# Splitting the second layer's messages into bf16 parts in a PSUM bank instead of in SBUF

## The reference

```python
Fj = features[src]                                  # gathered rows, 32 wide
R = relu(dist[:, None] @ w1 + b1) @ w2 + b2         # weights of every edge
acc += norm * einsum('euv,ef,evi,ofi->euo', Rb[..., k], Yf, Fb, C)
msg = concatenate(msg_blocks, axis=-1)
out = zeros(...).at[dst].add(msg)                   # sum at the destination
x = layernorm(x + out)
```

## Time and profile before

| | |
|---|---|
| median of 3 runs | 4053.04 us (4050.44 to 4053.18) |
| profiled execution | 4059.36 us |
| its span, first to last instruction | 4057.4 us |
| TensorE matmul busy | 3377.3 us (83%) |
| VectorE busy | 3460.9 us (85%) |
| GpSimd busy | 2953.0 us (73%) |
| ScalarE busy | 2184.8 us (54%) |
| GpSimd, gathers of the second layer | 1483.2 us in 1540 steps |
| VectorE, the 782 multiplies of the second layer | 832.4 us |

### The profile page before, as it was taken

How to read it: one execution, slowest core, us unless ns; L and a number is a source line. 1 busy time by engine, 2 the same in 40 slices (tenths; PEclk the granted TensorE clock), 3 DMA queues, 4 the chain that set the end, 5 groups by cost and what they waited for, 6 DMA issues and landing times. The chain is left out here.

```text
span 4057.4 us, 95500 instructions
## 1 busy us (share of the span) xinstructions
PE 3377.3 (83%) x23156; PEld 1945.7 (48%) x23156; DVE 3460.9 (85%) x5277; ACT 2184.8 (54%) x6587; POOL 2953.0 (73%) x3087
## 2 busy tenths in 40 slices
PE   4777777777777777777559999999999999999996
PEld 3444444444444444444335555555555555555553
DVE  8888888888888888888759999889889888988887
ACT  3555555555555555555335565555555555555554
POOL 5777777777777777777377777777777777777772
PEclk7888888888888888888779999999999999999998
DMA  3111111111111111111212222222221222222221
GB/s 107 35 33 32 34 32 33 34 33 35 32 33 32 33 32 34 36 32 33 35 38 48 45 44 44 44 44 44 47 45 41 47 44 44 44 43 44 44 44 28
DMA packets 238827, 162.68 MB, mean 40 GB/s; under 512 B 143937, under 2 KB 212594, under 8 KB 238066
## 3 DMA queue, kind: packets, MB, share of 16 engines
q1 hardware_dynamic: 104338, 91.78, 8.7%
q0 software_dynamic: 98560, 50.66, 8.6%
q10 hardware_dynamic: 35650, 17.88, 1.7%
HBM read 148.83 MB, written 10.43 MB: 39 GB/s over the span
## 5 line engine op out<-in xcount | busy, mean ns | idle before, releaser
L430 POOL DMA_INDIRECT rows<-x_rows,src x1540 | 1483.2, 963 | 536.6 <-issue 526.6
L430 POOL DMA_INDIRECT rows<-in_x,src x1540 | 1468.9, 954 | 485.6 <-issue 472.3
L775 PE MATMUL red<-prod,ident 128*128 128x336 f32 (+1 forms) x4704 | 1511.2, 475 | 1.4 <-DVE prod L1073 1.2
L775 PEld LDWEIGHTS red<-prod,ident 128*128 128x128 f32 x4704 | 892.3, 195 | 635.4 <-issue 193.3
L1073 DVE TENSOR_TENSOR prod<-wps,arena 128x896 f32<-128x896 f32 x782 | 832.4, 1083 | 176.2 <-PE wps L762 159.0
L755 PE MATMUL wps<-bias_parts,ones 64*128 64x448 bf16 (+1 forms) x2346 | 471.4, 398 | 610.7 <-DVE prod L1067 452.4
L565 ACT ACTIVATE gap<-iota,slot_plan 128x128 bf16<-128x128 f32 x3136 | 935.6, 386 | 7.0
L762 PE MATMUL wps<-w_sb,hidden 64*128 64x448 f32 (+1 forms) x3920 | 746.9, 476 | 0.0
L583 ACT ACTIVATE arena<-red 128x336 f32<-128x336 f32 (+1 forms) x294 | 135.5, 461 | 1103.5 <-PE red L775 1102.9
L755 PEld LDWEIGHTS wps<-bias_parts,ones 64*128 64x128 bf16 x2346 | 114.6, 94 | 1135.3 <-DVE prod L1067 562.4
L1082 DVE TENSOR_REDUCE arena<-prod 128x384 f32<-128x3072 f32 (+1 forms) x195 | 520.9, 2671 | 0.1
(11 more groups left out here) (127 smaller groups left out, 3025.3 us busy)
## 6 DMA issues: line engine op xcount, KB each, us to landing
mlp<-in_dist SPq DMA_DIRECT2D x196, 256.0 KB
fetched<-in_x SPq DMA_DIRECT2D x3072, 0.1 KB
fetched<-x_rows SPq DMA_DIRECT2D x3072, 0.1 KB
mlp<-in_feat SPq DMA_DIRECT2D x98, 256.0 KB
rows<-in_x,src POOLq DMA_INDIRECT x1540
rows<-x_rows,src POOLq DMA_INDIRECT x1540
frames<-frame ACTq DMA_DIRECT2D x49, 144.0 KB
geo<-frames ACTq DMA_DIRECT2D x98, 72.0 KB
```

The costliest lines, as they stand in the source:

```text
L430: nc.gpsimd.indirect_dma_start(out=rows[z][:, t, :], out_offset=None, in_=table_rows, in_offset=bass.IndirectOffsetOnAxis(ap=src_sb[z][:, ...
L775: ins = nc.tensor.matmul(red[:, bank * 512:bank * 512 + cols], ident[:], pr[:, i, :, a:b, :], start=(i == 0), stop=(i == MUL - 1))
```

## The change

For the second layer, except in the last round, the splits go through a PSUM bank. ScalarE copies the complete message into the bank `cut_ps` (512 columns, the whole of `acc`), VectorE subtracts the upper half in place there, ScalarE copies what is left to SBUF with a rounding to bf16 (`middle`, now the second part), and VectorE subtracts that from the bank to give the last part. ScalarE gains two copies a chunk and VectorE keeps two subtractions, of other operands. The scattered sums of the second layer move from `acc` to 128 free columns of the second bank of `red`; hence the scatter waits until both banks of sums are copied, and the second sum of products waits until the windows are split. In VectorE's order the first split moves from between windows 0 and 1 to behind multiply 6, and the second from behind multiply 6 to behind the projection, in the last round too (there they work in SBUF as before). The first layer keeps its order and its buffers.

```diff
+        red_end = 512 + (PE_SUMS[1][1][1] - PE_SUMS[1][1][0]) * PATHS[1] * MUL
+        acc_of = (acc[:, 0:GROUPS * FEAT], red[:, red_end:red_end + GROUPS * FEAT])
+        cut_ps = acc[:].rearrange("p (t f) -> p t f", t=TILES)
...
+        def middle(z):
+            return rest[z][:].bitcast(BF16)[:, :, 0:FEAT]
...
+            def copy_message(z, r, last):
+                s = layers[1]
+                if last:
+                    act.sem_inc(s.message_copied[z], 1)
+                    return
+                act.wait_ge(s.messages_ready[z], r + 1)
+                act.wait_ge(s.parts_ready[1 - z], r + z)
+                nc.scalar.activation(cut_ps, msg[z][:], ACT.Copy).then_inc(s.message_copied[z], 1)
+            def copy_middle(z, r, last):
+                s = layers[1]
+                if last:
+                    act.sem_inc(s.middle_ready[z], 1)
+                    return
+                act.wait_ge(s.rest_ready[z], r + 1)
+                nc.scalar.activation(middle(z), cut_ps, ACT.Copy).then_inc(s.middle_ready[z], 1)
...
                             hide(n, z, r + 1, 1)
+                        copy_message(z, r, last)
                         if not tail:
                             copy_sums(n, z1, r1, 0)
                             one_hots(n, z1, steps)
+                        copy_middle(z, r, last)
                         if not last:
                             copy_rows(n, i + 1, z, r + 1)
...
                 pe.wait_ge(s.sums_copied[1 - z], (r + z) * BANKS[n] - (BANKS[n] - 1 - bank))
+                if n == 1 and bank == 1:
+                    pe.wait_ge(s.windows_split[z], r)
...
                 pe.wait_ge(s.windows_split[1 - z], r + z)
-                cut = (upper(msg[z][:]), upper(rest[z][:]), last_part[z][:])
+                if n == 1:
+                    pe.wait_ge(s.sums_copied[1 - z], (r + z) * BANKS[1] + (0 if tail else BANKS[1]))
+                cut = (upper(msg[z][:]), middle(z) if n == 1 and not last else upper(rest[z][:]), last_part[z][:])
...
+                if not in_psum:
+                    dve.wait_ge(s.messages_ready[z], r + 1)
+                    whole, left = msg[z][:], rest[z][:]
+                else:
+                    dve.wait_ge(s.message_copied[z], r + 1)
+                    whole, left = cut_ps, cut_ps
+                nc.vector.tensor_tensor(left, whole, upper(msg[z][:]), ALU.subtract).then_inc(s.rest_ready[z], 1)
...
+                if not in_psum:
+                    dve.wait_ge(s.rest_ready[z], r + 1)
+                    left, part = rest[z][:], upper(rest[z][:])
+                else:
+                    dve.wait_ge(s.middle_ready[z], r + 1)
+                    left, part = cut_ps, middle(z)
+                nc.vector.tensor_tensor(last_part[z][:], left, part, ALU.subtract).then_inc(s.parts_ready[z], 1)
...
                 add_window(0, cols, z1, st)
-                cut_message(1, z, r)
                 add_window(1, cols, z1, st)
                 if not tail:
                     multiply(1, z1, r1, 5)
-                cut_rest(1, z, r)
+                cut_message(1, z, r, not last)
                 add_window(2, cols, z1, st)
                 if not last:
                     multiply(1, z1, r1, 6)
                     projected = project(1, i + 1, z, r + 1, st)
+                cut_rest(1, z, r, not last)
                 add_window(3, cols, z1, st)
```

More of the change, by code:

```diff
@@ L250, in __init__ @@
                 self.parts_ready = ring("parts_ready")
+                self.message_copied = ring("message_copied")
+                self.middle_ready = ring("middle_ready")
                 self.onehot_ready = ring("onehot_ready")
@@ L593, in split_windows @@
                         ins = nc.scalar.activation(split[z][:, g, w * FEAT:(w + 1) * FEAT],
-                                                   acc[:, g * FEAT:(g + 1) * FEAT], ACT.Identity,
+                                                   acc_of[n][:, g * FEAT:(g + 1) * FEAT], ACT.Identity,
                                                    scale=plan_sb[z][:, TILES + g * 2 + w:TILES + g * 2 + w + 1])
@@ L777, in sum_products, with scatter @@
                 ins.then_inc(s.products_summed[z], 1)
-            def scatter(n, z, r):
+            def scatter(n, z, r, last, tail):
                 s = layers[n]
@@ L788, in scatter @@
                     for part in range(3):
-                        ins = nc.tensor.matmul(acc[:, g * FEAT:(g + 1) * FEAT], onehot[z][:, t, :],
+                        ins = nc.tensor.matmul(acc_of[n][:, g * FEAT:(g + 1) * FEAT], onehot[z][:, t, :],
                                                cut[part][:, t, :], start=(tg == 0 and part == 0),
@@ L799, in body @@
                     if last and z == RING - 1:
-                        scatter(n, z, r)
+                        scatter(n, z, r, last, True)
                         pe.sem_inc(s.weights_ready[z], H - LAST_HALVES[n])
@@ L808, in body @@
                             sum_hidden(n, z, r + 1, 0)
-                        scatter(n, z, r)
+                        scatter(n, z, r, last, False)
                         if not last:
@@ L1083, in sum_tiles, with cut_message, cut_rest @@
                                                 products_oi(n)[:, :, 0:tiles - PE_TILES[n]], AX_X, ALU.add))
-            def cut_message(n, z, r):
+            def cut_message(n, z, r, in_psum=False):
                 s = layers[n]
-                dve.wait_ge(s.messages_ready[z], r + 1)
-                nc.vector.tensor_tensor(rest[z][:], msg[z][:], upper(msg[z][:]), ALU.subtract).then_inc(s.rest_ready[z], 1)
-            def cut_rest(n, z, r):
-                s = layers[n]
-                dve.wait_ge(s.rest_ready[z], r + 1)
-                nc.vector.tensor_tensor(last_part[z][:], rest[z][:], upper(rest[z][:]), ALU.subtract
-                                        ).then_inc(s.parts_ready[z], 1)
+                if not in_psum:
[5 more added lines that the diff above has]
+                nc.vector.tensor_tensor(left, whole, upper(msg[z][:]), ALU.subtract).then_inc(s.rest_ready[z], 1)
+            def cut_rest(n, z, r, in_psum=False):
+                s = layers[n]
+                if not in_psum:
[5 more added lines that the diff above has]
+                nc.vector.tensor_tensor(last_part[z][:], left, part, ALU.subtract).then_inc(s.parts_ready[z], 1)
             def project(n, i, z, r, st):
```

## The result

The changed kernel takes 4071.73 us (median of 5 runs, 4068.65 to 4072.89) against 4052.43 us for the kernel before (5 runs, 4048.22 to 4053.18): a ratio of 1.0049, 95% interval 1.0035 to 1.0064. It is slower by 19.3 us; a rise of 15.9 us to 4069 us was predicted. The two profiled executions lie 13.5 us apart (4072.89 and 4059.36 us), because the one of before was 7 us above its median.

A forecast was written before the change was run, and what follows sets the result against it. VectorE's chain (19.53 us a chunk) lay just under GpSimd's gather pace. Moved splits +49.0, gather waits -33.6, last round +0.5: +15.9 us on the profiled 4059.4 gives 4075.3, less 6.3 to the median, 4069 us; range 4038 to 4086.

The forecast's parts named there:

- What bounds the kernel: Second layer: VectorE's chain needs 19.53 us a chunk, GpSimd's gathers 20.1; gathers set the pace once their lead is gone.
- The price of the moved splits: Two splits moved in 96 chunk bodies: 0.60 us in 48 even ones, 0.42 in 48 odd ones, 49.0 us in all.
- the idle stretch: VectorE's wait for TensorE's sixth set of weights: loses 0.60 us of work and grows from 1.5 to 2.1 us a chunk.
- PSUM costs nothing: The two VectorE splits through PSUM: 0.60 us each on the chain, as in SBUF.
- The 65 ns a split: Alternative estimate from the skill's fixed costs for PSUM: each split 65 ns longer, 12 us in all; the prediction did not adopt it.
- The gain: Gathers shorten to 19.9 us a chunk, below VectorE's 20.04; 33.6 us of VectorE's waits for gathered rows vanish, nothing more.
- the 2.6 us that I gave to no gather: Over 95 chunks of the second layer, the part of the 36.2 us surplus beyond the 33.6 us of gather waits.
- The odd kind: Every other chunk body, 19.45 us: VectorE has 0.18 us to spare against TensorE, so only 0.42 of 0.60 us counts.
- ScalarE, the accumulator's bank, the queues: Two added copies a chunk (0.70 us each, 1.2 us slack), the scatter's new waits and unchanged transfers: no cost on the path.
- The end: Last round: in the last chunk the splits stand behind two more window additions, delaying the last scatter by about 0.5 us.
- The rival of cheap splits: Splits add under 0.16 us a chunk and GpSimd's relief of 18.6 us decides: 4034 us; chance 0.18 for below 4045.

The follow-up runs named there:

- fewer gathers: Second layer gathers at most 14 of 16 tiles a chunk: kernel before 4017.55 us (ratio 0.9915), changed kernel 4065.55 us (1.0036 to the same before).
- order-alone kernel: Kernel before with only VectorE's order changed, both splits in SBUF and one place on: 4072.18 us, ratio 1.0053; on the two slow chips 0.9936 and 0.9932.

## Why the prediction was right

- **What bounds the kernel.** VectorE's chain at 19.53 us under GpSimd's pace: right. With fewer gathers the chain shows at 19.53 us over the whole layer, and the time falls by 34 us, as the 33.6 us of waits said.
- **The price of the moved splits.** 49.0 us computed (48 x 0.60 + 48 x 0.42). Measured: 95 x (20.06 - 19.53) = 50 us in the changed kernel, 48.0 us between the two kernels with fewer gathers. Within it one step was wrong: the idle stretch was to grow from 1.5 to 2.1 us and grew to 1.88, because two window additions in a row, of which the second waits for the first, take 0.57 us and not 0.34. The prediction had seen that wait for the last round alone. The stretch is free, so the sum didn't feel it.
- **PSUM costs nothing.** Right by row (690 and 687 ns against 697 and 683) and by time: with the splits in SBUF the same order gives 4072.2 us, in PSUM 4071.7. The 65 ns a split that were estimated from the fixed costs in the Trainium skill (VectorE: DVE Perf Modes, "The TRN2 errata") are not there: the two PSUM forms together take 3 ns less than the two SBUF forms of the same order.
- **The gain.** 33.6 us of gather waits gone and nothing beyond: right. The wait line has vanished, and the relief of the gathers is visible in their steps and in no time. What the profiled pair had besides was the 2.6 us that I gave to no gather; it went too, so from the first to the 96th reduction 36.2 us stand against 50: 13.9 us net.
- **The odd kind.** 19.87 us computed, 19.90 measured. In the chunk before 2357.34 the last window addition takes 0.28 us instead of 0.22. It takes over 0.25 us in 36 of 48 odd chunks; beside 40 of the 48 a gather begins, and these average 0.27 us, the other 8 0.22. With fewer gathers odd chunks are at 19.86. That a gather holds up the addition, which reads two inputs in SBUF, fits, and was not isolated: in even chunks a gather begins beside 41 of 47, and only 7 take that long.
- **ScalarE, the accumulator's bank, the queues.** None of VectorE's waits names them. Right; the slack of the two copies was 2.0 and 1.7 us, where 1.2 was computed.
- **The end.** 0.5 us foreseen for the last chunk, 0.36 measured (from the 98th reduction to the end 30.85 us instead of 30.49). Not foreseen were 0.57 us between the 96th and the 97th reduction (24.07 us instead of 22.90, of which 0.60 is the split), where the third multiply waits 0.49 us for weights, which it does not in the kernel before.
- **The size.** 15.9 us against a measured 19.3. The working was against one profiled execution, which was 7 us above its median; against that pair 13.5 us were measured. By the medians the sum was 3.4 us short, by the pair 2.4 us too high. So it is in part luck that 4069 lies within 3 us of the result. Why that execution was late is not settled: its second layer began 2 us later and had the 2.6 us above.
- **The rival of cheap splits** was wrong on this kernel and right as a mechanism: its 4034 us appear, at 4036.0, once one split is off the chain.

## What to carry to other kernels

Price a moved instruction by where it lands, not by its length: 0.60 us in a stretch that ends on another engine's result costs nothing, and the same 0.60 us behind that result costs it in every turn. When two limits lie close to each other, relief for one is worth only as much as the other leaves: the shorter gather steps went with a gain of 14 us with VectorE's chain at 19.53 us a chunk, and gained nothing with it at 20.06. And measure the pace in a stretch where the slower limit isn't yet at work, such as the start of a loop that begins with data in store: it gives the second limit before any experiment.

## What the runs showed of the hardware

Two of five chips used for the experiments ran the kernel before in 6765 and 6761 us (medians of 15 and 14 runs, 6737 to 6797), the three others in 4050.4 to 4051.4. The page of the order-alone kernel on the first of them, groups by line (busy, mean ns, idle before):

```profile
L789 PE MATMUL acc<-last_part,onehot 128*128 128x32 bf16 x3136 | 327.3, 182 | 689.4 <-issue 689.0
L789 PE MATMUL acc<-msg,onehot 128*128 128x32 bf16 x3136 | 326.4, 182 | 660.1 <-issue 651.8
```

Its scatter matmuls take 182 ns, where the same page on a usual chip has 177, but TensorE stands idle 2000 us in front of them in the two layers (these two rows and a third alike), almost all of it put down to issue; in the stretch from 4500 to 6000 us the longest such pause in front of a scatter matmul is 2.7 us. GpSimd waited 1354 us in the second layer for index loads. The mean granted clock was 0.756 instead of 0.91. The trace names no cause; that instructions and small transfers reached the core late fits both lines, and was not tested. A kernel's ratio on such a chip says nothing of its limits on the others: the order alone was 0.7% faster there and 0.5% slower elsewhere.

A VectorE subtraction of 512 elements that reads and writes a PSUM bank in place takes what the SBUF form takes (690 and 697 ns), and ScalarE's copy of 512 elements takes 0.58 us into PSUM and 0.60 out of it. Of the gather instructions that begin in the first 0.5 us of a split with two SBUF inputs, 50 of 51, 36 of 60 and 60 of 64 are drawn out, from 0.94 to as much as 1.47 us (kernel before, order alone, fewer gathers). The 25 exceptions of the first two all begin in the first 33 ns of the split, and no gather that begins 36 ns to 0.4 us behind its start escapes. Beside a split that has one of its inputs in PSUM none is drawn out, in 131 cases of two kernels, of which 102 begin later than 34 ns. The second of two window additions in a row starts 0.35 us behind the first (mean of 101 pairs in the changed kernel), where a split starts 0.13 us behind such an addition (2510.26 and 2510.39). In the program an addition waits until the one before is done; the split has no such wait.
